# A four-layer gated attention network on one Trainium2 core: the load of turned queries and keys moves ahead of the store of probabilities on SyncE

## The reference, cut to what matters

```
for layer in 0..3:
    x = x + tanh(g_xattn[layer]) * attention[layer](layernorm(x), ctx)
    x = x + tanh(g_ffn[layer])   * ffn[layer](layernorm(x))

attention 0, 1, 3 (8 groups of 4 query heads, 128 dims each):
    q = xn @ Wq;  k = ctx @ Wk;  v = ctx @ Wv
    layer 0: q, k rotated by position;   layers 1, 3: q, k rmsnorm'd over 128 dims
    p = softmax(q k^T / sqrt(128) + mask);   out = (p v) @ Wo
attention 2: 32 small heads of 16 dims
ffn 0: base + low-rank experts; 1: a dequantised matrix; 2: top-2 of 16 experts + shared; 3: one of 8 experts
```

## Time and profile before

| | |
|---|---|
| median of 3 runs | 2883.64 us (2881.02 to 2886.97) |
| the profiled execution | 2890.32 us, span 2888.5 us |
| PE busy | 2438.5 us, 84% of the span |
| PE weight load busy | 1996.1 us, 69% |
| DVE busy | 1860.4 us, 64% |
| POOL busy | 1553.4 us, 54% |
| ACT busy | 1213.2 us, 42% |
| mean granted TensorE clock | 0.935 of full speed |
| chain that ended last, largest part | DMA 10% of the span, q_in<-between_q 6% |

### The profile page before, as it was taken

One profiled execution on the slowest core, in us unless ns is written; L12 is line 12 of the kernel. 1 busy time (PEld: TensorE's weight loads), 2 busy tenths in 40 slices (PEclk: granted clock), 3 DMA queues, 4 the chain that ended last, 5 costly groups with the idle time before them and its releaser, 6 DMA issues. The chain is left out here.

```text
span 2888.5 us, 40547 instructions
## 1 busy us (share of the span) xinstructions
PE 2438.5 (84%) x12225; PEld 1996.1 (69%) x12225; DVE 1860.4 (64%) x3505; ACT 1213.2 (42%) x3610; POOL 1553.4 (54%) x1624
## 2 busy tenths in 40 slices
PE   5888888888888888889788888799788888889877
PEld 4777777676677777777666677676567777777753
DVE  4766666666887666666676676563376666666762
ACT  2433333333424455555542445323235555555420
POOL 4565565565424566666542666541446666666433
PEclk8998888889999999999999999899889999999989
DMA  3345555555313444444431000148624444444254
GB/s 103 94 157 176 169 194 172 177 172 172 126 63 116 156 147 146 148 150 149 139 128 45 16 1 1 42 161 310 241 63 138 149 152 152 148 142 144 93 194 164
DMA packets 296365, 390.33 MB, mean 135 GB/s; under 512 B 20977, under 2 KB 195697, under 8 KB 293210
## 3 DMA queue, kind: packets, MB, share of 16 engines
q1 hardware_dynamic: 280416, 338.60, 36.1%
q0 software_dynamic: 10224, 42.03, 4.2%
q10 hardware_dynamic: 5514, 7.11, 0.8%
HBM read 269.92 MB, written 151.49 MB: 146 GB/s over the span
## 5 line engine op out<-in xcount | busy, mean ns | idle before, releaser
L2252 POOL TENSOR_TENSOR qT_l<-q_in,qT_h 128x512 fp32r<-128x512 f32 x156 | 203.6, 1305 | 380.1 <-ACT qT_h L1197 379.3
L898 PE MATMUL B_s<-kT,qT_h 128*128 128x256 f32 x768 | 215.9, 358 | 174.5 <-POOL qT_l L2252 151.4
L1376 ACT ACTIVATE W<-S,nmx 128x128 f32<-128x128 f32 x768 | 297.6, 393 | 63.6 <-DVE nmx L1703 63.3
L1522 DVE TENSOR_TENSOR oT_l<-B_three,oT_h 128x512 fp32r<-128x512 f32 x200 | 137.2, 686 | 285.5 <-ACT oT_h L1197 285.3
L898 PEld LDWEIGHTS B_s<-kT,qT_h 128*128 128x128 f32 x768 | 154.8, 202 | 229.1 <-POOL qT_l L2252 198.7
L2292 POOL TENSOR_TENSOR W<-W,rden 128x512 f32<-128x512 f32 x192 | 200.1, 1042 | 204.9 <-DVE rden L1708 204.8
L841 PE MATMUL B_out<-ring_h,oT_h 128*128 128x512 f32 x516 | 230.6, 447 | 40.7 <-DVE oT_l L1522 34.8
L1197 ACT ACTIVATE q_in<-q_in,wqk 128x128 f32<-128x128 f32 x104 | 55.2, 531 | 488.2 <-DMA q_in<-between_q 488.2
L1718 DVE STREAM_TRANSPOSE S<-W 128x512 f32<-128x512 f32 x184 | 130.6, 710 | 188.0 <-POOL W L2292 187.8
L2298 POOL TENSOR_TENSOR pT_l<-W,pT_h 128x512 fp32r<-128x512 f32 x184 | 238.6, 1297 | 21.3 <-ACT pT_h L1197 21.2
L2228 POOL TENSOR_TENSOR ring_l<-raw,ring_h 128x512 fp32r<-128x512 f32 x166 | 214.3, 1293 | 62.7 <-ACT ring_h L1197 62.6
(11 more groups left out here) (504 smaller groups left out, 7901.3 us busy)
## 6 DMA issues: line engine op xcount, KB each, us to landing
raw<-in_pieces SPq DMA_DIRECT2D x270, 256.0 KB
between_q<-xn SPq DMA_DIRECT2D x156, 320.0 KB, 2.9
q_in<-between_q SPq DMA_DIRECT2D x156, 320.0 KB, 3.2
between_p<-S SPq DMA_DIRECT2D x184, 256.0 KB, 2.1
W<-between_p SPq DMA_DIRECT2D x184, 256.0 KB, 3.0
slots_x<-in_zero SPq DMA_DIRECT2D x32, 1030.0 KB, 5.9
raw<-in_experts SPq DMA_DIRECT2D x16, 768.0 KB, 7.3
w<-in_experts SPq DMA_DIRECT2D x8, 1024.0 KB, 15.9
```

Of the source, the lines that this page charges most:

```text
L898: pe.matmul(B_s[:, cols(r, 2 * P)], qT[0][:, cols(r)], kT_both[:, :], start=True, stop=False)
L1376: t = act.activation(probs_r, scores_r, ACT.Exp, bias=nmx[:, k, r:r + 1], accum_out=den[:, k, r:r + 1])
L1522: return dve.tensor_tensor(dst, a, b, ALU.subtract)
L2252: pool.tensor_tensor(heads_first(qT[1][:, :]), queries_in, heads_first(f32(qT[0][:, :])), ALU.subtract).then_inc(*q_low.now((layer, u)))
```

## The change

One due time is changed: `load_q` of unit U1 stands at place 41 of its iteration and no longer at 72. The steps of the same iteration that lie between the two places are `store_p` of U3 (42), in layer 0 `clear_slots` (47), and loads of weights that are forced at place 70; for the first two units of each layer also `load_p` of the units whose probabilities are stored at place 21 (62). Only SP issues anything for `load_q`, so the streams of PE, DVE, ACT and POOL are the same instructions in the same order.

```diff
@@ -157,7 +157,7 @@
                 self.at(i + 1, 12, "store_q", layer, u)
-                self.at(i + 1, 72, "load_q", layer, u)
+                self.at(i + 1, 41, "load_q", layer, u)
                 self.at(i + 2, 13, "split_k", layer, u)
```

## The result

The changed kernel takes 2629.89 us (median of 4 runs, 2624.47 to 2640.73), the kernel before 2882.33 us in the same comparison (2877.57 to 2886.97). The ratio is 0.913, 95% interval [0.909, 0.917]: 8.7% faster. The forecast was 2650, with a range of 2600 to 2750. The profiled execution took 2624.64 us, its span is 2622.8 us against 2888.5: 265.7 us less.

What follows compares the result with a forecast made beforehand. The q_in load behind store_p, which waits for S, was taken to set the period in layers 1 and 3; in layer 0 the clear also stood ahead. Gains 125 + 108 = 233 us gave 2650 us, range 2600 to 2750.

Steps and rivals of the forecast that it cites:

- The loop through store_p: Layers 1 and 3: q_in load, S, store_p's issue and the next load close a 10.49 us loop that is the period.
- The gain of layers 1 and 3: Period falls from 10.32 to 9.0 us over 95 iterations: 125 us gained, ends 97 and 149.
- Which loop: Period after: TensorE 8.74 us, queries' round trip 8.7 per iteration, or one q_in tile's loop 7.8, which doesn't bind.
- TensorE's own 8.74: Layers 1 and 3: TensorE's work per iteration with both its waits gone, the first of three possible bounds.
- The round trip: Queries from ScalarE's start on q_in through S, transpose, store and load: 17.4 us over two iterations, 8.7 per iteration.
- Layer 0: Period falls from 11.52 to 9.4 us over 51 iterations: 108 us gained, ends 72 and 131.
- store_p's issue isn't held up: The q_in load, now ahead of store_p, goes out before S is ready (2412.3 against 2414.54).
- the slower rival: Probabilities come late and ScalarE waits at pT_h for W: 2953 us, chance 0.03.
- The VectorE rival: VectorE's low part of kT falls into GpSimd's work and delays oT_l: 2729 to 2777 us, chance 0.13.
- The rest: Units 8 and 9 of each layer, other stretches, layer 2 and feed-forward parts: no gain.
- The signs: Layer 3 loads about 9 us apart, before S; q_in wait under 350 us; layer 0 clock 0.95; layer 3 TensorE about 1.0.

Runs made afterwards that it cites:

- e2: Kernel before with the q_in load moved to place 41 in layers 1 and 3 alone, at 72 in layer 0: 2730.5 us, ratio 0.946.
- e3: Kernel before with the q_in load at place 43 in all layers, behind store_p but ahead of layer 0's clear: 2785.6 us, ratio 0.964.
- e5: Kernel before with the q_in load at place 74, behind load_p, which waits until store_p has landed: 3222.5 us, ratio 1.113.
- e7: Changed kernel without the product of xn's low part with Wq's high part, 4 matmuls fewer per turned unit: 2630.9 us.
- e6: Changed kernel with VectorE's mask steps in layers 1 and 3 moved behind the normalisation and block transpose of the queries: 2842.2 us.
- e4: Changed kernel with the 32 clears issued in layer 2 instead of in every second iteration of layer 0: 2610.6 us.
- e1: Kernel before with the q_in load moved to place 41 in layer 0 alone, at 72 in layers 1 and 3: 2797.9 us, ratio 0.969.
- e11: Changed kernel with the first weight split of steady iterations at place 43, not 15, and 4 query-projection matmuls fewer per turned unit: 2646.6 us.
- e13: Changed kernel with layer 0's clear behind load_p (place 74), not between store_p and load_p (47): 2674.0 us.

## Why the prediction was right, and where it wasn't

*The loop through store_p.* Right. Shown by e2, e3 and e5: layers 1 and 3 follow the load's place relative to the store, in both directions. The forecast of 2650 missed 2630 by 20 us. In the profiled executions 266 us were gained where 233 were forecast: 21 more in layers 1 and 3, 9 fewer in layer 0, and 21 outside, so only the 9 hid part of an error.

*The gain of layers 1 and 3.* Forecast 125 us (period 9.0), measured 72.4 + 73.5 = 146 (8.77 and 8.81). The sum of the loops, 8.7, was the better number; my 9.0 put in 0.3 us for loops taking turns, a choice and not a sum of rows, and 0.1 was right.

*Which loop.* Half right. I put TensorE's own 8.74 first. The round trip and TensorE are so near each other that the period alone can't tell them apart, and TensorE's row looks full. Less TensorE work (e7) tells: TensorE is level with the bound but isn't it. The round trip is: its parts come to 17.54 us with hardly a wait in them. I also missed the loop through GpSimd and VectorE (8.71, in some iterations) and the loop of mask and exp, on which e6 ran aground.

*Layer 0.* Forecast 108 us (9.4), measured 98.9 (9.58). I named the late store of the queries, and its landing (200 to 600 us) was 3.7 us in the median where I took 3.1:

```profile
slots_x<-in_zero SPq DMA_DIRECT2D x21, 1030.0 KB, 7.5
...
between_q<-xn SPq DMA_DIRECT2D x41, 320.0 KB, 3.7
q_in<-between_q SPq DMA_DIRECT2D x41, 320.0 KB, 3.3
```

The kernel before has 3.4 us in the same window; the 3.1 of the earlier trace rows come from 400 to 640 us. And a loop adds up means, not medians: over 49 round trips of layer 0 the landing took 3.83 us, the way from S to the end of the block transpose 5.66 where I had 5.29, the load 3.43 where I had 3.27, and the sum is 19.2 where I had 17.9 to 20.2. The load of q_in lands in 3.3 us in the median (row above), as forecast; in the earlier trace rows it took about twice that.

*"store_p's issue isn't held up."* Right in layers 1 and 3, wrong in layer 0. There SyncE stands at load_q for the landing of the query store behind the clear, and store_p stands behind it. Timeline of the changed kernel (start us, us, instruction):

```profile
307.91 0.32 SPq L2450 DMA_DIRECT2D between_q<-xn  x1
...
310.61 0.71 DVE L1718 STREAM_TRANSPOSE S<-W 128x512 f32<-128x512 f32 x1 [1.16 <-POOL W L2292]
...
311.54 0.63 ACT L1197 ACTIVATE pT_h<-W 128x512 fp32r<-128x512 f32 x1 [2.89 <-DMA W<-between_p]
...
312.32 0.37 SPq L2463 DMA_DIRECT2D q_in<-between_q  x1
312.78 0.46 SPq L2437 DMA_DIRECT2D between_p<-S  x1
```

S is done at 311.32, and store_p goes at 312.78. Between 210 and 630 us 22 of 43 stores go more than 0.3 us late, by 1.4 us on average; before, none did. Together with W behind the clear (ScalarE waits for it at pT_h, 2.89 us here) this is the slower rival's mechanism, in layer 0 alone. Its price is small and not measured by itself: e4 takes it away together with the late landings of the queries' store and gains 24 us, and those landings make up 0.93 of the 0.95 us by which its round trip is shorter.

*The VectorE rival.* Its mechanism came true and most of its price didn't. The low part of kT (ns min/median/max, first and last start), against the earlier trace rows:

```profile
L1522 DVE TENSOR_TENSOR kT<-q_in,kT x156: 339/767/1436, 139.2 to 2451.8; 128x128 fp32r<-128x128 f32 x156
```

The median doubled, from 383 to 767 ns; the mean went from 0.54 to 0.74 us, under the 0.9 that was named as the sign. The timeline of e7 above shows one case. In the changed kernel's timeline in the first section it starts at 2212.16 inside GpSimd's ring_l and ends at 2213.22, 0.16 us behind that one's end at 2213.06. That agrees with the Trainium skill (SBUF — State Buffer, section "Who interferes with whom"), which has VectorE's second SBUF input wait for GpSimd's read interface. It cost little because the subtraction mostly had room: oT_l behind it waits for oT_h anyway. But not always: in layers 1 and 3 oT_l starts 0.19 and 0.21 us after the end of oT_h in the mean, 0.97 at most, where the kernel before has 0.03 throughout; the way from ScalarE's start to the end of S grew as much in layer 3, from 6.56 us in the mean to 6.78. That stands once in a round trip of two iterations, so 0.08 us per iteration, 8 us in all, is an estimate of its price from these rows; no run takes it away.

*The rest.* 21 us that I counted as nothing. Loads of weights that are forced at place 70 now stand behind the load of q_in. e3, which passes them and not store_p, has 18 us outside the three stretches, e2 13 and e1 -3, so most of it seems to come without passing store_p in the loop; with executions that lie up to 16 us apart the shares are not shown.

*The signs.* Loads 8.8 us apart and ahead of S, a clock of 1.00 in layer 0 and TensorE busy for 0.98 of layer 3 came as named. ScalarE's wait for q_in fell to 466 us and not under 350: in a loop without slack the engine still waits for the load, only for less time.

## What to carry to other kernels

When a chain of waits repeats once per iteration, add it up from one issue to the next: if the sum is the period, the edit that opens it is worth the distance to the next longest loop, so work out all the others first, also those that close over two iterations, and with the mean of each part. An instruction that waits in an in-order queue passes its wait on to all behind it; a transfer that is ready early belongs ahead of one that is ready late, and a large one without a deadline belongs where no loop stands behind it (32 clears moved into layer 2 gave 24 us in layer 0 and cost 7 elsewhere). A full row of an engine does not prove it is the bound; take some of its work away and see.

## What was not expected of the hardware

- The 320 KB store of queries has no one landing time. Its mean was 2.7 us in layer 3 before and after, 3.1 in e11 with the same transfers per iteration in another order, 3.5 in layer 0 before, 3.8 after and 4.7 in e13. What stands near it in the queue differs between these; which neighbour costs what no run shows.
- The granted clock was 0.89 in layer 0 before and 1.00 after, 0.98 and 1.00 in layers 1 and 3, with the same TensorE instructions. It goes with the load's place: layer 0 has 1.00 in e1 and 0.89 in e2. TensorE's waits of up to 5 us in front of the scores (under 1 us after) seem to have cost clock beside their own time; no run separates the two.
- An idle time that the profile puts down to one engine can be another's: GpSimd's 0.93 us "for rden" above began with a VectorE subtraction that took 1.06 us beside GpSimd's weight split, and 0.38 in the median of the kernel before.
